# A graph layer on one core: the order of a load queue, of one rounding, and the engine that rounds the weights

## The chip, the core and the metric

The program runs on one core of a Trainium2 chip. The core has a matrix engine (TensorE, PE in the profile), three engines for work on whole tiles (VectorE is DVE, ScalarE is ACT, GpSimd is POOL) and SyncE (SP), which here only issues transfers. Each engine works through its own list in order; semaphores tie the lists together. Sixteen DMA engines move data between memory (HBM) and the on-chip buffers; the matrix engine writes into eight banks of PSUM. The metric is the device time of one execution in microseconds: of the kernel before, the median of 3 runs.

## What is computed

There are 16 batches, each with 512 nodes of 128 features (`x`) and a weighted adjacency matrix `adj` of 512x512. Seven relations are formed: the matrix, twice (relations 0 and 1), its transpose, twice (3 and 4), a shift by one node and its transpose (2 and 5), and the identity (6). The output is the largest of the seven, plus a bias and the input.

```python
h = jnp.maximum(_layernorm(x, axis=-1), 0.0)
...
HW = jnp.einsum('bnf,rfo->rbno', features, W[:, :F]) + jnp.einsum('rd,rdo->ro', W_edges, W[:, F:])[:, None, None, :]
AHW = jnp.einsum('rbnm,rbmo->rbno', A, HW)
out = jnp.max(AHW, axis=0) + b
return out
```

The term of `W_edges` is one vector per relation, c. Under a matrix A it becomes the row sums (or, for the transpose, the column sums) of A times c.

## The kernel before, in words

Every fp32 product is made of three products of rounded parts: each operand is split into a rounded `hi` and the rest `lo`, and `passes` (L847 to L849) multiplies hi by hi, lo by hi, hi by lo. ACT makes nearly every `hi` (for A, A turned, h turned, and the two products `fwd` and `bwd`), DVE or GpSimd the `lo`. The weights of the seven relations have `w_hi` and `w_lo`: the first three places are those of relations 2, 5 and 6 (`EYE`), the other four those of `FWD` (0, 1) and `BWD` (3, 4).

For a batch, `fwd` is the product of the turned A with h and `bwd` that of A with h, each over four chunks of 128 nodes. The three relations of `EYE` need only the turned h. The four others are finished a batch later, within the next batch's work (`along`, on PE): ACT first fills a bank with the sums of A times c (`fill`, L492), and the product with the weights is added onto it. DVE joins each finished relation into `best` (L669, L672), the first one by ACT (`join_first`, L500); then `best` is turned back and GpSimd adds bias and input.

The sums of A come as a by-product of ACT's rounding, as columns. PE turns them (L844), ACT writes them into `sum_rows` (`take_sums`, L487), SP stores them in memory (`store_sums`, L258, 4 KB) and reads them back spread over all 128 partitions (`spread_sums`, L264, 512 KB into `sum_all`). `fill` waits for this spread. There are two sets of buffers; batch b uses set b mod 2, and (k, q) in the code is batch 2k + q.

SP's queue carries all that is loaded in the regular part: x of a later batch (L212, 256 KB), the same x by blocks of 32x32 (`xp_sb`, L216, four transfers of 64 KB), blocks of the last column chunk of A (`a_blocks`, L216, four of 64 KB), A itself (`reload_a`, L245, two of 512 KB, for the batch two later), and the stores of the result (L221, four of 64 KB). The order is written out by hand: `first_steps` for batches 0 and 1, then `step` for every batch.

The order of ACT's and GpSimd's work is written out by hand as well, in a `first_step` (batch 0) and a `step` with special cases for batch 1 (`second`). In batch 1's step ACT rounds `bwd` of batch 0 only behind two fills and the normalisation of batch 2 (L462). The weights are rounded by ACT in `first_step` (L504), in two pieces, and split by GpSimd (L377).

Of the kernel before, what the change touches and what calls it, by code (L numbers as in the profile page):

```python
# [6 lines left out]
def gnn_layer(nc, x, adj, W, W_edges, bias, out):  # L7
# [15 lines left out]
    ACT = mybir.ActivationFunctionType  # L23
# [23 lines left out]
    with ctx:  # L47
# [162 lines left out]
        def _(sp):  # L210
# [22 lines left out]
            def load_xp(k, q):  # L233
                wait(sp, xb_ready, 2 * k + q - 1)
                load_by_blocks(xp_sb[q], x[2 * k + q, :, :], xp_loaded[q])
# [13 lines left out]
            def load_a_blocks(k, q):  # L249

                b = 2 * k + q
                wait(sp, a_turned[C - 1], b - 3)
                load_by_blocks(a_blocks[q], adj[b, :, (C - 1) * P:], a_blocks_loaded[q])

            def store_sums(k, q):

                sp.wait_ge(sum_rows_ready, 2 * k + q + 1)
                sp.dma_start(sums_dram[q][:, :], sum_rows[q][:]).then_inc(sums_stored[q], 16)  # L258
# [20 lines left out]
            def first_steps():  # L279

                load_x(0, 0)
                load_a(0, 0, 1)
                load_a(0, 0, 3)

                sp.wait_ge(a_loaded[0][0], 16)
                load_x(0, 1)
                load_w(EYE[:1], w_loaded)
                load_w(EYE[1:], w_loaded)
                for j in range(C):
                    load_a(0, 1, j)  # L290
                load_w(FWD, w_rest_loaded)
                load_w(BWD, w_rest_loaded)
                reload_x(0, 0)
                reload_a(0, 0)
                store_sums(0, 0)
                load_a_blocks(1, 0)
                spread_sums(0, 0)
                reload_x(0, 1)
                load_by_blocks(bias_sb, bias, bias_loaded)
                load_xp(0, 0)  # L300
                load_a_blocks(1, 1)
                load_xp(0, 1)
                store_sums(0, 1)
                reload_a(0, 1)
                spread_sums(0, 1)

            def step(k, q, more):

# [26 lines left out]
        def _(pool):  # L335
# [36 lines left out]
                wait(pool, out_stored[q], G * 16 * k)  # L372
                pool.tensor_tensor(o_sb[q][:], turned[q][:], xb_sb[q][:], ALU.add).then_inc(out_ready, 1)  # L373

            def split_w(n, places):
                pool.wait_ge(w_hi_ready, n + 1)
                pool.tensor_tensor(w_lo[:, places, :], w_sb[:, places, :], w_hi[:, places, :].bitcast(fp32),  # L377
                                   ALU.subtract).then_inc(w_lo_ready, 1)

            def first_step():  # L380
                ahead = (0, 1)
                split_a(0, 0, 2)
                split_a(0, 0, 3)
                reciprocal_std(*ahead)
                split_w(0, slice(0, W_EYE))
                split_h(*ahead)

            def step(k, q, left):
                if is_batch(2 * k + q, 1):
                    split_w(1, slice(W_EYE, R))  # L390
                    reciprocal_std(*after(k, q))
                    split_a(k, q, 0)
                    split_a(k, q, 1)
                    split_a(k, q, 2)
                    split_a(k, q, 3)
                    pool.wait_ge(bias_loaded, G * 16)
                else:
                    if left:
                        reciprocal_std(*after(k, q))
                    split_a(k, q, 2)  # L400
                    split_a(k, q, 3)
                    finish(k - 1, q)
                add_bias(*before(k, q))
                if left:
                    ahead = after(k, q)
                    split_h(*ahead)
                    split_a(*ahead, 0)
                    split_a(*ahead, 1)
# [23 lines left out]
        def _(act):  # L432
# [45 lines left out]
            def round_bwd(k, q):  # L478
                b = 2 * k + q
                act.wait_ge(bwd_done, b + 1)  # L480
                wait(act, rel_done[BWD[-1]], b)
                act.activation(bwd_hi[:], bwd_ps[:], ACT.Copy).then_inc(bwd_hi_ready, 1)
# [17 lines left out]
                act.activation(best[q][:], rel_bank(b, r)[:], ACT.Identity,  # L500
                               bias=c_col[:, r:r + 1]).then_inc(joined[r], 1)

            def round_w(places):
                act.activation(w_hi[:, places, :], w_sb[:, places, :], ACT.Copy).then_inc(w_hi_ready, 1)  # L504

            def first_step():
                ahead = (0, 1)
                act.wait_ge(w_loaded, 2 * 16)
                round_w(slice(0, W_EYE))
                take_sums(0, 0, rel_ps[1])  # L510
                round_at(*ahead, 0)
                round_at(*ahead, 1)
                normalise(*ahead)
                round_fwd(0, 0)
                act.wait_ge(c_ready, 1)
                join_first(0, 0)
                round_at(*ahead, 2)
                round_ht(*ahead)
                act.wait_ge(w_rest_loaded, 2 * 16)
                round_w(slice(W_EYE, R))  # L520
                round_at(*ahead, 3)
                round_a(*ahead, 0)
                round_a(*ahead, 1)

            def step(k, q, left):
                b = 2 * k + q
                prev = before(k, q)
                second = is_batch(b, 1)
                if not second:
                    round_at(k, q, 2)  # L530
                    round_at(k, q, 3)
                join_first(k, q)
                if not second:
                    take_sums(k, q)
                if second:
                    act.wait_ge(joined[EYE[1]], b)
                else:
                    act.wait_ge(joined[BWD[0]], b - 1)
                fill(*prev, FWD[0], rel_ps[BANK[FWD[0]]], filled[FWD[0]])
                act.wait_ge(joined[EYE[0]], b + 1)  # L540
                fill(*prev, FWD[1], rel_ps[BANK[FWD[1]]], filled[FWD[1]])
                if left:
                    ahead = after(k, q)
                    normalise(*ahead)
                if second:
                    round_bwd(*prev)
                    round_a(k, q, 2)
                    round_a(k, q, 3)
                act.wait_ge(joined[FWD[0]], b)
                fill(*prev, BWD[0], rel_ps[BANK[BWD[0]]], filled[BWD[0]])  # L550
                if left:
                    round_at(*ahead, 0)
                    if second:
                        take_sums(k, q, rel_ps[1])
                else:
                    round_fwd(k, q)
                act.wait_ge(joined[FWD[1]], b)
                fill(*prev, BWD[1], rel_ps[BANK[BWD[1]]], filled[BWD[1]])
                if left:
                    round_at(*ahead, 1)  # L560
                    round_ht(*ahead)
                    round_fwd(k, q)
                    for j in range(C):
                        round_a(*ahead, j)
                    round_bwd(k, q)
# [458 lines left out]
```

## Time and profile before

| | before |
|---|---|
| runs | 217.28, 215.5, 214.74 us; median 215.5 |
| profiled execution | 218.58 us, of which the span is 216.7 |
| PE busy | 205.2 us (95%) |
| DVE busy | 187.9 us (87%) |
| ACT busy | 186.6 us (86%) |
| GpSimd busy | 171.7 us (79%) |
| mean granted clock of PE | 0.985 |
| moved by DMA | 42.38 MB, mean 196 GB/s |

The profile is of one execution. Times in its rows count from the start of its span, in us. The granted clock is the share of 2.4 GHz that PE was given: 1.00, or 0.50, which is 1.2 GHz, and values between are means over a stretch. What a row has in brackets is the engine's idle time just ahead of the first instruction in it, and what ended it. A transfer's "landing" is the time from its issue to its arrival. The median lies 3.1 us below the profiled execution.

### The profile page before, as it was taken

How to read it: one execution, taken by the hardware profiler on the slowest of the kernel's cores; microseconds unless marked ns; L12 is line 12 of the kernel's file. 1: busy time of each engine (PE TensorE's matmuls, PEld its weight loads, DVE VectorE, ACT ScalarE, POOL GpSimd, SP SyncE). 2: the span in 40 equal slices, each digit the busy share in tenths (PEclk: the TensorE clock that was granted, in tenths of full speed). 3: DMA queues.
4: the chain of work that ended last, by engine and by line, in shares of the span. 5: the costliest groups of instructions: out<-in, count | busy, mean ns of one | idle time of the engine just before them, and what ended most of it. 6: DMA issues, size and time to landing. Idle time of an engine off the chain costs nothing.

```text
span 216.7 us, 4978 instructions
## 1 busy us (share of the span) xinstructions
PE 205.2 (95%) x1013; PEld 167.0 (77%) x1013; DVE 187.9 (87%) x400; ACT 186.6 (86%) x469; POOL 171.7 (79%) x181
## 2 busy tenths in 40 slices
PE   7799989799999999999999999999999999999980
PEld 5588865587888888788888888888888888888860
DVE  4798399389899989899899989999899989979783
ACT  4799887698999999999999999999999999999550
POOL 1566879829799797979899797979889797979341
PEclk9999999699999999999999999999999999999997
DMA  6997879796897989989888989899897989062726
GB/s 226 313 304 169 118 143 292 97 316 129 230 219 178 249 145 297 169 246 193 214 234 156 269 149 327 154 308 170 260 198 177 259 177 245 8 153 38 165 33 93
DMA packets 120320, 42.38 MB, mean 196 GB/s; under 512 B 100743, under 2 KB 110071, under 8 KB 120311
## 3 DMA queue, kind: packets, MB, share of 16 engines
q1 hardware_dynamic: 118688, 41.57, 80.0%
q10 hardware_dynamic: 1623, 0.71, 1.2%
q8 instruction: 3, 0.05, 0.1%
q14 instruction: 6, 0.05, 0.1%
HBM read 38.00 MB, written 4.26 MB: 195 GB/s over the span
## 4 chain that ended last, share of the span: by engine, by line
PE 79%; DMA 7%; SPq 5%; DVE 3%; ACT 2%; POOL 1%; issue 1%; DVEq 0%; ACTq 0%; POOLq 0%
PE rel_ps L849 11%; PE rel_ps L847 10%; PE rel_ps L848 10%; PE at_ps L821 8%; PE bwd_ps L847 6%; PE bwd_ps L849 6%; PE bwd_ps L848 6%; PE fwd_ps L847 6%; PE fwd_ps L849 6%; PE fwd_ps L848 6%; SPq L216 5%; DMA sum_all<-sums_dram 3%; DMA sums_dram<-sum_rows 3%; PE turn_ps L832 3%; DMA x_sb<-in_x 1%
## 5 line engine op out<-in xcount | busy, mean ns | idle before, releaser
L351 POOL TENSOR_TENSOR a_lo<-a_sb,a_hi 128x512 fp32r<-128x512 f32 x62 | 81.1, 1328 | 23.1 <-ACT a_hi L439 23.1
L672 DVE TENSOR_TENSOR best<-rel_ps,best 128x512 f32<-128x512 f32 x62 | 42.4, 684 | 6.8 <-PE rel_ps L849 5.7
L492 ACT ACTIVATE rel_ps<-sum_all,c_col 128x512 f32<-128x512 f32 (+1 forms) x63 | 41.6, 673 | 6.7 <-DVE best L672 4.1
L439 ACT ACTIVATE a_hi<-a_sb 128x512 fp32r<-128x512 f32 x64 | 39.6, 633 | 2.1 <-DMA a_sb<-in_adj 2.1
L643 DVE TENSOR_TENSOR at_lo<-at_ps,at_hi 128x512 fp32r<-128x512 f32 x48 | 32.8, 686 | 3.3 <-ACT at_hi L452 2.5
L452 ACT ACTIVATE at_hi<-at_ps 128x512 fp32r<-128x512 f32 x48 | 28.3, 591 | 5.0 <-PE at_ps L821 5.0
L847 PE MATMUL bwd_ps<-a_hi,h_hi 128*128 128x512 f32 x64 | 26.6, 416 | 1.4 <-DVE h_hi L760 0.8
L366 POOL TENSOR_TENSOR xb_sb<-xp_sb,bias_sb 128x512 f32<-128x512 f32 x16 | 23.0, 1436 | 5.2 <-DMA xp_sb<-in_x 5.2
L847 PE MATMUL fwd_ps<-at_hi,h_hi 128*128 128x512 f32 x64 | 26.8, 419 | 0.0
L821 PEld LDWEIGHTS at_ps<-ident,a_sb 128*128 128x128 f32 x184 | 22.2, 142 | 4.2 <-issue 0.2
L849 PE MATMUL fwd_ps<-at_hi,h_lo 128*128 128x512 f32 x64 | 25.4, 397 | 0.0
L821 PE MATMUL at_ps<-ident,a_sb 128*128 128x128 f32 x184 | 25.3, 273 | 0.0
L669 DVE SCALAR_TENSOR_TENSOR best<-rel_ps,c_col,best 128x512 f32<-128x512 f32 x32 | 23.8, 744 | 1.7 <-PE rel_ps L849 1.5
L848 PE MATMUL fwd_ps<-at_lo,h_hi 128*128 128x512 f32 x64 | 25.2, 394 | 0.0
L849 PE MATMUL bwd_ps<-a_hi,h_lo 128*128 128x512 f32 x64 | 25.2, 394 | 0.0
L848 PE MATMUL bwd_ps<-a_lo,h_hi 128*128 128x512 f32 x64 | 25.0, 391 | 0.0
L462 ACT ACTIVATE h_sb<-x_sb,shift,rstd 128x128 f32<-128x128 f32 x60 | 24.6, 479 | 0.0
L359 POOL TENSOR_TENSOR h_lo<-h_sb,h_hi 128x512 fp32r<-128x512 f32 x15 | 19.4, 1295 | 2.9 <-DVE h_hi L637 2.9
L847 PE MATMUL rel_ps<-ht_hi,w_hi 128*128 128x512 f32 x48 | 20.2, 421 | 0.0
L373 POOL TENSOR_TENSOR o_sb<-turned,xb_sb 128x512 f32<-128x512 f32 x15 | 19.7, 1315 | 0.0
L849 PE MATMUL rel_ps<-ht_hi,w_lo 128*128 128x512 f32 x48 | 19.0, 396 | 0.0
L848 PE MATMUL rel_ps<-ht_lo,w_hi 128*128 128x512 f32 x48 | 19.0, 395 | 0.0
(105 smaller groups left out, 471.7 us busy)
## 6 DMA issues: line engine op xcount, KB each, us to landing
a_sb<-in_adj SPq DMA_DIRECT2D x28, 512.0 KB, 4.2
sum_all<-sums_dram SPq DMA_DIRECT2D x16, 512.0 KB, 5.7
x_sb<-in_x SPq DMA_DIRECT2D x16, 256.0 KB, 5.0
xp_sb<-in_x SPq DMA_DIRECT2D x64, 64.0 KB, 2.9
out<-o_sb SPq DMA_DIRECT2D x60, 64.0 KB, 4.8
a_blocks<-in_adj SPq DMA_DIRECT2D x56, 64.0 KB, 2.3
a_sb<-in_adj SPq DMA_DIRECT2D x6, 256.0 KB, 4.3
a_sb<-in_adj ACTq DMA_DIRECT2D x2, 256.0 KB, 3.7
```

The costliest lines, as they stand in the source:

```text
L351: pool.tensor_tensor(a_lo[q][:, j, :], a_sb[q][:, j, :], a_hi[q][:, j, :].bitcast(fp32), ALU.subtract).then_inc(a_lo_ready[j], 1)
L439: act.activation(a_hi[q][:, j, :], a_sb[q][:, j, :], ACT.Copy, accum_out=sums[q][:, 0, j:j + 1]).then_inc(a_hi_ready[j], 1)
L452: act.activation(at_hi[q][:, i, :], at_from(b, i)[:], ACT.Copy, accum_out=sums[q][:, 1, i:i + 1]).then_inc(at_hi_ready[i], 1)
L462: last = act.activation(h_sb[q][:, j, :], x_sb[q][:, j, :], ACT.Relu, bias=shift[q][:, j:j + 1], scale=rstd[q][:, j:j + 1])
L492: act.activation(to[:, cols], sum_all[q][:, 0 if r in FWD else 1, cols], ACT.Copy, scale=c_col[:, r:r + 1]).then_inc(after_it, 1)
L643: dve.tensor_tensor(at_lo[q][:, i, :], at_from(b, i)[:], at_hi[q][:, i, :].bitcast(fp32), ALU.subtract).then_inc(at_lo_ready[i], 1)
L669: dve.scalar_tensor_tensor(out=best[q][:], in0=held[:], scalar=c_col[:, r:r + 1], in1=best[q][:], op0=ALU.add, op1=ALU.max).then_inc(joine ...
L672: dve.tensor_tensor(best[q][:], held[:], best[q][:], ALU.max).then_inc(joined[r], 1)
L821: last = pe.transpose(at_from(b, i)[:, j * P:(j + 1) * P], a_sb[q][:, j, i * P:(i + 1) * P], ident[:])
L847: pe.matmul(out, w_hi_, m_hi, start=start, stop=False, skip_group_check=onto)
L848: pe.matmul(out, w_hi_, m_lo, start=False, stop=False, skip_group_check=onto)
L849: return pe.matmul(out, w_lo_, m_hi, start=False, stop=stop, skip_group_check=onto)
```

## The change

Three edits are made, all for batches 0 and 1.

1. In SP's `first_steps`, the store of batch 1's sums goes ahead of the blocks of batch 3, and the spread ahead of the reload of A for batch 3; the load of xp of batch 1 goes last.
2. In ACT's step of batch 1, the rounding of batch 0's `bwd` moves from behind the fills and the normalisation to just behind the first join of batch 1.
3. The two roundings of the weights move from ACT to GpSimd, where each stands directly ahead of the split that uses it; GpSimd takes over the wait for the load.

```diff
@@ SP, first_steps
                 load_xp(0, 0)
+                store_sums(0, 1)
                 load_a_blocks(1, 1)
+                spread_sums(0, 1)
+                reload_a(0, 1)
                 load_xp(0, 1)
-                store_sums(0, 1)
-                reload_a(0, 1)
-                spread_sums(0, 1)
@@ GpSimd
-            def split_w(n, places):
+            def split_w(n, places, loaded):
+                pool.wait_ge(loaded, 2 * 16)
+                pool.tensor_copy(w_hi[:, places, :], w_sb[:, places, :]).then_inc(w_hi_ready, 1)
                 pool.wait_ge(w_hi_ready, n + 1)
                 pool.tensor_tensor(w_lo[:, places, :], w_sb[:, places, :], w_hi[:, places, :].bitcast(fp32),
                                    ALU.subtract).then_inc(w_lo_ready, 1)
...
-                split_w(0, slice(0, W_EYE))
+                split_w(0, slice(0, W_EYE), w_loaded)
...
-                    split_w(1, slice(W_EYE, R))
+                    split_w(1, slice(W_EYE, R), w_rest_loaded)
@@ ACT, first_step
-            def round_w(places):
-                act.activation(w_hi[:, places, :], w_sb[:, places, :], ACT.Copy).then_inc(w_hi_ready, 1)
-
...
-                act.wait_ge(w_loaded, 2 * 16)
-                round_w(slice(0, W_EYE))
                 take_sums(0, 0, rel_ps[1])
...
                 round_ht(*ahead)
-                act.wait_ge(w_rest_loaded, 2 * 16)
-                round_w(slice(W_EYE, R))
@@ ACT, step
                 if second:
+                    round_bwd(*prev)
                     act.wait_ge(joined[EYE[1]], b)
...
                 if second:
-                    round_bwd(*prev)
                     round_a(k, q, 2)
                     round_a(k, q, 3)
```

SP's queue, at the end of `first_steps` (`sums_dram<-sum_rows` is the store of the sums, `sum_all<-sums_dram` the spread, all three from batch 1; `a_blocks` and `a_sb` are for batch 3; the first `xp_sb` is batch 0's, the last batch 1's):

```order
 L216 DMA xp_sb<-in_x 32x16x32 x4
+L258 DMA sums_dram<-sum_rows 8x128
 L216 DMA a_blocks<-in_adj 32x16x32 x4
+L264 DMA sum_all<-sums_dram 128x1024
+L245 DMA a_sb<-in_adj 128x2x512 x2
 L216 DMA xp_sb<-in_x 32x16x32 x4
-L258 DMA sums_dram<-sum_rows 8x128
-L245 DMA a_sb<-in_adj 128x2x512 x2
-L264 DMA sum_all<-sums_dram 128x1024
```

The store has moved past two groups of four transfers, the spread past xp and A, and A past xp.

ACT's list before, from the rounding of h turned for batch 1 to the fill of the first bank of batch 0's transposed relations (`best1` is batch 1's join, `rel_ps` the banks filled with batch 0's sums, `h_sb0` batch 2's normalisation):

```order
22 L470 ACTIVATE ht_hi1<-turn_ps 128x512
23 L504 ACTIVATE w_hi<-w_sb 128x512
24 L452 ACTIVATE at_hi1,sums1<-at_ps1 128x512
25 L439 ACTIVATE a_hi1,sums1<-a_sb1 128x512 x2
26 L500 ACTIVATE best1<-rel_ps0,c_col 128x512
27 L492 ACTIVATE rel_ps2<-sum_all0,c_col 128x512
28 L492 ACTIVATE rel_ps0<-sum_all0,c_col 128x512
29 L462 ACTIVATE h_sb0<-x_sb0,shift0,rstd0 128x128 x4
30 L482 ACTIVATE bwd_hi<-bwd_ps 128x512
31 L439 ACTIVATE a_hi1,sums1<-a_sb1 128x512 x2
32 L492 ACTIVATE rel_ps2<-sum_all0,c_col 128x512
```

And the same piece in the changed kernel:

```order
21 L472 ACTIVATE ht_hi1<-turn_ps 128x512
22 L454 ACTIVATE at_hi1,sums1<-at_ps1 128x512
23 L441 ACTIVATE a_hi1,sums1<-a_sb1 128x512 x2
24 L502 ACTIVATE best1<-rel_ps0,c_col 128x512
25 L484 ACTIVATE bwd_hi<-bwd_ps 128x512
26 L494 ACTIVATE rel_ps2<-sum_all0,c_col 128x512
27 L494 ACTIVATE rel_ps0<-sum_all0,c_col 128x512
28 L464 ACTIVATE h_sb0<-x_sb0,shift0,rstd0 128x128 x4
29 L441 ACTIVATE a_hi1,sums1<-a_sb1 128x512 x2
30 L494 ACTIVATE rel_ps2<-sum_all0,c_col 128x512
```

The rounding of the weights is gone, and `bwd_hi` has moved ahead of two fills and the normalisation. The roundings of the weights now stand in GpSimd's list as `CAST w_hi<-w_sb`, of 128x384 and 128x512, each ahead of `w_lo<-w_sb,w_hi`.

## Rows read from the trace of the kernel before

**Rows 1.** Busy us (count) by stretch; then granted clock, DMA share, GB/s:

```profile
40.00:50.00 10.00, 10.00 (x47) 8.21 (x46) 7.40 (x19) 7.87 (x22) 5.62 (x7) 0.84 0.83 215
50.00:100.00 50.00, 50.00 (x254) 41.23 (x253) 46.76 (x98) 46.97 (x119) 44.51 (x46) 1.00 0.89 210
```

**Rows 2.** Chain that ended last, pieces: start us, us, what:

```profile
31.84 6.56 DMA sum_all<-sums_dram
...
55.45 0.87 PE at_ps L821 x8
...
67.72 0.87 PE at_ps L821 x8
```

**Rows 3.** Timeline near 39 us: start, us, engine, line, operation:

```profile
38.49 1.30 ACT L492 ACTIVATE rel_ps<-sum_all,c_col 128x512 f32<-128x512 f32 x2 [2.03 <-DMA sum_all<-sums_dram]
...
39.23 0.50 PE L847 MATMUL rel_ps<-fwd_hi,w_hi 128*128 128x512 f32 x1 [1.77 <-ACT rel_ps L492]
```

**Rows 4.** Timeline, 21 to 30 us, of ACT, DVE and PE:

```profile
21.23 0.69 ACT L500 ACTIVATE best<-rel_ps,c_col 128x512 f32<-128x512 f32 x1
...
25.23 0.69 DVE L660 TENSOR_TENSOR bwd_lo<-bwd_ps,bwd_hi 128x512 fp32r<-128x512 f32 x1 [3.36 <-ACT bwd_hi L482]
...
27.81 0.69 ACT L492 ACTIVATE rel_ps<-sum_all,c_col 128x512 f32<-128x512 f32 x1 [1.38 <-DVE best L672]
...
28.55 0.50 PE L847 MATMUL rel_ps<-bwd_hi,w_hi 128*128 128x512 f32 x1 [0.77 <-ACT rel_ps L492]
...
29.01 0.25 ACT L487 ACTIVATE sum_rows<-rel_ps 8x128 f32<-8x128 f32 x1
```

**Rows 5.** Timeline: PE's first turns of A for batches 2 and 3:

```profile
25.19 1.04 PE L821 MATMUL at_ps<-ident,a_sb 128*128 128x128 f32 x8
...
42.86 1.17 PE L821 MATMUL at_ps<-ident,a_sb 128*128 128x128 f32 x8
```

**Rows 6.** Timeline, 13 to 20 us, of the weights' splits and what is near:

```profile
13.51 1.01 POOL L377 TENSOR_TENSOR w_lo<-w_sb,w_hi 128x384 fp32r<-128x384 f32 x1
...
16.21 0.40 PE L847 MATMUL rel_ps<-ht_hi,w_hi 128*128 128x512 f32 x1
...
16.51 0.41 DVE L637 CAST h_hi<-h_sb 128x512 fp32r<-128x512 f32 x1
...
19.52 1.29 POOL L377 TENSOR_TENSOR w_lo<-w_sb,w_hi 128x512 fp32r<-128x512 f32 x1 [1.25 <-ACT w_hi L504]
```

**Rows 7.** Timeline of SP's queue: issue starts, and us until issued:

```profile
24.46 3.10 SPq L216 DMA_DIRECT2D a_blocks<-in_adj  x4
...
33.23 4.75 SPq L216 DMA_DIRECT2D xp_sb<-in_x  x4
...
43.14 0.39 SPq L264 DMA_DIRECT2D sum_all<-sums_dram  x1
...
46.48 2.61 SPq L212 DMA_DIRECT2D x_sb<-in_x  x1
...
92.98 0.35 SPq L264 DMA_DIRECT2D sum_all<-sums_dram  x1
```

**Rows 8.** Waits of SP, 45 to 60 us: total, times, longest:

```profile
SPq L264 <- DMA sums_dram<-sum_rows: 0.3, 1, 0.3
```

**Rows 9.** Landing (last column, us) of the spreads issued 17.71, 43.14, 92.98:

```profile
sum_all<-sums_dram SPq DMA_DIRECT2D x1, 512.0 KB, 4.0
...
sum_all<-sums_dram SPq DMA_DIRECT2D x1, 512.0 KB, 6.1
...
sum_all<-sums_dram SPq DMA_DIRECT2D x1, 512.0 KB, 6.7
```

**Rows 10.** Timeline: use of the sums of batches 2 and 6:

```profile
52.18 1.28 ACT L492 ACTIVATE rel_ps<-sum_all,c_col 128x512 f32<-128x512 f32 x2
...
101.25 1.28 ACT L492 ACTIVATE rel_ps<-sum_all,c_col 128x512 f32<-128x512 f32 x2
...
102.27 0.39 PE L847 MATMUL rel_ps<-fwd_hi,w_hi 128*128 128x512 f32 x1
```

## What I expected, written before the changed kernel ran

> **What bounds the kernel now.** I read the page's busy times, the table of stretches, the chain that ended last, and then the timeline at the one place where that chain leaves the matrix engine. PE is busy for 95% of the span, and from 50 to 100 us for every microsecond, at the full clock [rows 1]. One batch follows another every 12.27 us (PE's turns of A start at 55.45 and at 67.72 [rows 2]). So from batch 2 on (batches count from 0) the kernel runs at PE's pace, and what PE loses before that shows in full at the end. The chain names the loss: the spread sums of batch 1 are issued at 31.84 and land 6.56 us later [rows 2]. ACT waits 2.03 us for them and PE 1.77 us for ACT [rows 3]. A second loss follows: after this idle time PE works at 1.2 GHz. From 40 to 50 us the mean grant is 0.84 [rows 1], so 3.2 us of it were at a grant of 0.5, which cost 1.6 us; some of it lies just before 40, I take 1.75. A third lies ahead: DVE waits 3.36 us for `bwd_hi`, which ACT rounds late; DVE's joins are late by it, so ACT waits 1.38 us for the join before it fills a bank, and PE 0.77 us for that bank [rows 4].
>
> These come to 1.77 + 1.75 + 0.77 = 4.3 us. Another count: PE's turns of A start at 25.19 and 42.86 [rows 5], 17.67 us apart where the regular step is 12.27: 5.4 too long. I take 4.7, between the two.
>
> **The change part by part.**
>
> *bwd rounded first.* The product that is rounded has long been done. ACT can round it behind its first join of batch 1, which ends at 21.9 [rows 4], until 22.5; DVE's split moves from 25.23 to 22.5. From that split to the join that ACT waits for DVE needs 25.23 to 27.8 now [rows 4], 2.6 us, so the join is there at 25.1, or 25.4 since PE's product for it comes only then. ACT reaches the fill at 26.4, as early as it does now, and no longer waits: 1.3 us gained on ACT. `sum_rows` of batch 1, written from 29.01 to 29.26 now [rows 4], is there at 28.0. PE loses its 0.77. The price is 0.6 us on the fills of batch 0's forward banks, for the first of which PE then waits 0 to 0.1 us, and on the normalisation of batch 2, which PE's turns of A (from 25.19 [rows 5], 0.9 us of work) hide.
>
> *Weights rounded on GpSimd.* ACT loses two pieces of work of about 0.6 us. The first is worth nothing, as ACT then waits for PE's turned sums, the second little, as ACT then waits for PE's first relation of batch 1. GpSimd gets two CASTs, and no row of this kernel shows one. Bounds: DVE's cast of 128x512 takes 0.41 us, which scaled to 384 columns is 0.3; GpSimd's two-operand pass over the same 128x384 takes 1.01 [rows 6]. I take 0.8, nearer to the row of the same engine. It starts where that pass starts now, 13.51, so `w_lo` is ready at 13.51 + 0.8 + 1.01 + 0.1 = 15.4. PE's product is at 16.21, its weight load 0.2 before [rows 6]: hidden by 0.6 us, a stall from a cast of 1.4 us on. The second CAST, by the same bounds 0.4 to 1.35 us, falls into the 1.25 us that GpSimd now waits for ACT's rounding ahead of 19.52 [rows 6]: nothing.
>
> *The queue.* Before, SP issued blocks, xp, sums, A (2 x 512 KB), spread. Now it stands from 24.46 [rows 7], where it issued blocks, until `sum_rows` at 28.0; it issues the blocks by 30.5 and the spread at 30.6 instead of 31.84, with no A ahead. The spread took 6.56 us behind 1 MB of A [rows 2], and 4.0 for batch 0 without it [rows 9]. I take 4.3: landed at 34.9 instead of 38.4. ACT could have used it at 36.5 in the old kernel and is 1.0 ahead of that now, 35.5. **So the stall and the fall of the clock behind it go, and PE is 4.7 us ahead at batch 2.** A for batch 3 now goes at 31.2 behind the sums. PE turns it at 38.1 (42.86 less 4.7); with 0.5 MB ahead of it, it has 7 us. The batch 1 spread, with twice that ahead, took 6.56: I take no wait, up to 0.5 us as the bound.
>
> *What becomes late next.* SP's rows decide how much of the 4.7 stays. The spread of batch 2 is issued at 43.14 [rows 7] and takes 6.1 us [rows 9]: 49.24. The load of x behind it is issued at 46.48 and holds SP for 2.61 us, until 49.09 [rows 7], just when the spread has landed. Yet of waits for semaphores SP shows 0.3 us there [rows 8]. So SP is held by full queues, and its round is a loop of its own: spread landed, x, xp, blocks, sums, A, spread. It does not go faster because PE does. How far ahead is it? Batch 2's sums land at 49.24 and are used at 52.18 [rows 10]: 2.9 us. Batch 6's go at 92.98 [rows 7], land 6.7 later [rows 9] at 99.68, and ACT uses them at 101.25. Its two fills take 1.28, so the first ends at 101.9, and PE wants it at 102.27 [rows 10]: 1.57 + 0.35 = 1.92 us is all that PE can be ahead there, and it is the least of the batches that I read; for batch 2 it is 3.3. **So of 4.7 us 1.92 stay, plus what the queue itself gains.**
>
> That has bounds. If SP is never held, it issues x of batch 4 at 34.3, xp without the 4.75 us of [rows 7], and the spread of batch 2 at 41.0: 2.1 us earlier. If it is held as long as now, everything from x on is some 1.7 us later (it stands 3.6 us, and has 2 us of issues fewer in front of the sums). I take 0.4 us earlier, near the middle. **Kept: 1.9 + 0.4 = 2.3 us.** The profiled execution's own time, 218.58 us (span 216.7 and 1.9 around it), becomes 216.3. It lies 3.1 us above the median of the three runs, 215.5. I take the same 2.3 off that: 213.2, a ratio of 0.989. About 1% (213.35 to 217.65) is what a measurement of this kernel can tell from no change.
>
> By the rows of the spread, 6.56 behind A and 4.0 without, the transfers pass in order of issue. The Trainium skill has the rule ("DMA: Bandwidth & Descriptors", Queues, rings and completion order): on each DMA engine descriptors are consumed in ring order. By it whatever goes behind the sums pays for them, which speaks against a free gain; its result would be the 1.7 us bound, 215.3.
>
> **The rivals.**
> 1. *The queue keeps up* (17%). Against it: x's issue ends with the landing. For it: the DMA engines are busy for 0.89 of the time [rows 1], not all. Then 4.2 to 4.7 us stay: 210.8 to 211.3.
> 2. *The clock falls again* (12%). When PE catches up with the queue in batch 2, it idles 4.7 - 3.3 - 0.4 = 1.0 us, between the 0.77 us behind which the trace shows no slower product and the 1.77 us behind which it fell to 1.2. A fall costs 1.75 us, after which PE is late enough not to catch up soon: at worst 2.3 - 1.75 = 0.6 us kept, 214.9.
> 3. *The queue comes out late* (9%), at its bound: 1.9 - 1.7 = 0.2 us kept, 215.3.
> 4. *Slower* (7%): the cast is dear. Were it 4 us, `w_lo` would come at 18.6, PE would stall 2.6 us and probably run at half rate behind it (1.75 us more), and the sums and the queue would move by as much: 2.3 - 4.35 = 2.0 us lost, 217.5. It stalls from 1.4 us on; the sign turns at about 2 us with a fall of the clock, else at 3.7. For it speaks only that no row shows the operation. "GPSIMD Engine Reference" of the Trainium skill, Engine selection, says one-input operations run roughly at line rate there, which no row shows.
>
> **How the numbers follow.** The forecast has 55%, alone 211.8 to 214.9: the queue's move to either side of 0.4 by 1 us, and some noise. Faster by over 1%: its better part, 33%, and rival 1, 17%: 50%. Within 1%: its rest, 22%, and rivals 2 and 3: 43%. Slower by over 1%: 7%, the heavy forms of rival 4 and what I don't see. The range goes from rival 1's 210.8 to just above rival 3's, 215.5.
>
> **What would show it.** In the changed profile: DVE's split of bwd near 22.5, no wait of 1.38 us on ACT; `sum_rows` of batch 1 near 28.0; its spread issued near 30.6, landed near 35; a full clock and no idle PE from 35 to 45, and its turns of A near 38.2. Then ACT or PE waits for `sum_all` in batches 2 to 8, 0.2 to 1 us each, which were not there; SP's spread of batch 2 between 41.0 and 44.8. Wrong would be: CASTs over 1.4 us and a wait of PE for `w_lo`, a grant of 0.5 near 50 us, or no new wait for `sum_all` at all.

## The result, and the profile after

The change made the kernel slower: 219.96 us against 216.05 us, medians of four runs each (218.03 to 221.21 against 214.74 to 217.28), a ratio of 1.016 with an interval of 1.010 to 1.021. Forecast were 213.2 us and a gain of 1%. Ratios, here and below, are of fast runs: those over 1.5% above their kernel's fastest are left out, so that a ratio needn't be the quotient of the two medians.

The table sets beside each other the two profiled executions and the medians. It has a trap: both profiles lie off their kernel's middle, and in opposite directions. That of before, which the forecast read, lies 2.5 us over its median, that of after 1.9 us under its own. By the two profiles alone the change gains 0.5 us.

| | before | after |
|---|---|---|
| median of the runs | 216.05 us | 219.96 us |
| profiled execution, span | 218.58, 216.7 us | 218.03, 216.2 us |
| PE busy | 205.2 us | 203.9 us |
| clock of that execution | 0.985 | 0.998 |
| clocks of the changed kernel's other three runs | | 0.989, 0.983, 0.976 |

The stall of batch 1 is gone. This is the changed kernel's timeline, by the columns of [rows 3]: ACT fills the banks of batch 1 with no wait ahead of it, and PE turns A for batch 3.

```profile
35.98 1.28 ACT L494 ACTIVATE rel_ps<-sum_all,c_col 128x512 f32<-128x512 f32 x2
...
39.11 1.06 PE L816 MATMUL at_ps<-ident,a_sb 128*128 128x128 f32 x8
```

PE's turns come 3.75 us earlier than in [rows 5]. A batch later stands a longer stall than the one that went:

```profile
51.64 1.30 ACT L494 ACTIVATE rel_ps<-sum_all,c_col 128x512 f32<-128x512 f32 x2 [3.23 <-DMA sum_all<-sums_dram]
...
52.38 0.50 PE L842 MATMUL rel_ps<-fwd_hi,w_hi 128*128 128x512 f32 x1 [2.89 <-ACT rel_ps L494]
```

In the kernel before ACT used these sums at 52.18 without a wait [rows 10]. The chain that ended last (start, us, what) now goes through their spread, and then PE's beat takes over, 12.26 us where [rows 2] had 12.27. Ahead of the spread the chain runs through SP's own issues, so it is SP's queue and not an engine that sets the time there:

```profile
32.76 0.47 SPq L216
...
36.75 1.88 SPq L212
...
41.63 1.39 SPq L216
...
46.27 5.29 DMA sum_all<-sums_dram
51.64 0.70 ACT rel_ps L494
52.38 0.50 PE rel_ps L842
...
54.73 0.87 PE at_ps L816 x8
...
66.99 0.87 PE at_ps L816 x8
```

The stretches, with the columns of [rows 1], show PE idle for 2.4 us between 50 and 55 (and 0.5 just before), and the clock full in this execution:

```profile
40.00:50.00 10.00, 9.49 (x47) 7.43 (x45) 9.64 (x23) 7.81 (x22) 8.53 (x11) 1.00 0.86 192
50.00:55.00 5.00, 2.62 (x13) 2.18 (x14) 1.29 (x3) 3.36 (x7) 3.42 (x3) 1.00 1.06 233
```

The spread of batch 2 was issued at 43.14 before [rows 7], and is issued at 46.27 now. SP's queue in the changed kernel (issue starts, us until issued):

```profile
21.57 4.02 SPq L216 DMA_DIRECT2D xp_sb<-in_x  x4
28.90 0.28 SPq L258 DMA_DIRECT2D sums_dram<-sum_rows  x1
29.22 1.90 SPq L216 DMA_DIRECT2D a_blocks<-in_adj  x4
31.17 0.49 SPq L264 DMA_DIRECT2D sum_all<-sums_dram  x1
31.82 0.90 SPq L245 DMA_DIRECT2D a_sb<-in_adj  x2
32.76 3.60 SPq L216 DMA_DIRECT2D xp_sb<-in_x  x4
36.75 1.88 SPq L212 DMA_DIRECT2D x_sb<-in_x  x1
38.88 1.92 SPq L216 DMA_DIRECT2D xp_sb<-in_x  x4
41.10 3.33 SPq L216 DMA_DIRECT2D a_blocks<-in_adj  x4
44.49 0.38 SPq L258 DMA_DIRECT2D sums_dram<-sum_rows  x1
45.13 1.02 SPq L245 DMA_DIRECT2D a_sb<-in_adj  x2
46.27 0.39 SPq L264 DMA_DIRECT2D sum_all<-sums_dram  x1
```

From 25.59, where the first xp has been issued, to 28.90 SP stands, and the profile's waits of SP name what for:

```profile
SPq L258 <- ACT sum_rows L489: 3.3, 1, 3.3
```

Two theories were to be told apart. **The late queue**: the store stands ahead of eight transfers that were ready; while SP waits for the sums these aren't issued, and afterwards there is no slack in which to catch up, so the spread of batch 2 is late by that much. **The clock**: PE's new idle time makes the clock fall in most executions, and PE's half rate behind it is the loss. (In the expectations Q is the late queue, and E the rival that the edits of the engines bring the loss; L and C are the late queue alone, and the clock beside it.)

### The profile page after: what moved, and what is told of

It is laid out like the page before. It is cut to its first block, busy times and chain, and to the rows that moved or that the text cites. A ratio compares the mean times of both kernels' runs of the same rounds, so it can differ in the third digit from the quotient of the medians.

```text
span 216.2 us, 4978 instructions
## 1 busy us (share of the span) xinstructions
PE 203.9 (94%) x1013; PEld 166.3 (77%) x1013; DVE 188.3 (87%) x400; ACT 185.3 (86%) x467; POOL 172.5 (80%) x183
## 4 chain that ended last, share of the span: by engine, by line
PE 76%; SPq 7%; DMA 5%; DVE 4%; ACT 3%; issue 3%; ACTq 0%; DVEq 0%
PE rel_ps L842 10%; PE rel_ps L844 10%; PE rel_ps L843 10%; PE at_ps L816 8%; PE fwd_ps L842 6%; PE fwd_ps L844 6%; PE fwd_ps L843 6%; PE bwd_ps L842 6%; PE bwd_ps L844 6%; PE bwd_ps L843 6%; SPq L216 4%; PE turn_ps L827 3%; DMA sum_all<-sums_dram 2%; DMA a_sb<-in_adj 2%; SPq L212 1%
```

## The experiments

Ratios are to the kernel before on the same chip, with 95% intervals. "Store to spread" is the time on SP from the issue of batch 1's store to the issue of batch 2's spread. "Turns" is the start of PE's turns of A for batch 4. These two, the issue of the spread and the span are of one profiled execution, the median clock is that of all runs of the row. The clock of an execution also counts its last microseconds, in which PE has nothing left to do (from 210 us on 0.75 in the profile of before), so 0.990 is only a rough line between executions in which it fell in the work and those in which it didn't.

| kernel | median us | ratio | median clock | store | store to spread | spread of batch 2 | turns | span |
|---|---|---|---|---|---|---|---|---|
| before, profile of rows 1 to 10 | 216.05 | 1 | | 29.74 | 13.40 | 43.14 | 55.28 | 216.7 |
| `e11_before_again` | 216.52 (one run) | | 0.996 | 29.17 | 12.94 | 42.11 | 53.21 | 214.6 |
| after | 219.96 | 1.0157 (1.0100 to 1.0214) | 0.986 | 28.90 | 17.37 | 46.27 | 54.58 | 216.2 |
| `e3_changed_again` | 220.21 | 1.0137 (1.0082 to 1.0192) | 0.9865 | 27.55 | 18.06 | 45.61 | 56.55 | 218.9 |
| `e1_queue_alone` | 221.40 | 1.0126 (1.0083 to 1.0169) | 0.9885 | 29.04 | 18.20 | 47.24 | 57.88 | 219.3 |
| `e2_engines_alone` | 217.91 | 1.0032 (0.9996 to 1.0068) | 0.9865 | 29.53 | 13.42 | 42.95 | 55.45 | 216.9 |
| `e4_swap_only` | 217.03 | 0.9988 (0.9949 to 1.0028) | 0.9925 | 29.08 | 14.50 | 43.58 | 52.46 | 213.9 |
| `e5_no_wait_for_sums` | 216.55 | 0.9953 (0.9915 to 0.9991) | 0.9925 | 25.87 | 17.43 | 43.30 | 53.90 | 215.5 |
| `e6_xp_fills_the_wait` | 216.51 | 0.9996 (0.9956 to 1.0035) | 0.9915 | 27.66 | 14.95 | 42.61 | 51.79 | 214.2 |
| `e7_fill_idle_slots` | 215.56 | 0.9929 (0.9895 to 0.9962) | 0.993 | 29.47 | 13.89 | 43.36 | 52.61 | 214.1 |
| `e12_fill_again` | 215.68 | 0.9918 (0.9878 to 0.9958) | 0.992 | 29.96 | 14.34 | 44.30 | 53.67 | 215.1 |
| `e10_filled_old_engines` | 216.41 | 0.9977 (0.9950 to 1.0005) | 0.993 | 29.09 | 14.09 | 43.18 | 52.97 | 214.4 |
| `e9_changed_kept_warm` | 218.44 | 1.0114 (1.0074 to 1.0153) | 0.996 | 27.66 | 16.66 | 44.32 | 55.05 | 216.7 |
| `e8_xp_as_long_rows` | 215.94 | 0.9953 (0.9914 to 0.9993) | 0.994 | 29.44 | 15.85 | 45.29 | 54.24 | 215.7 |

One regularity helps in reading it: span less turns is 161.4 to 161.7 in twelve of the fourteen profiles, and 162.4 in the two others (`e3_changed_again`, `e6_xp_fills_the_wait`). From batch 4 on the kernel is nearly the same in all of them. What differs happens ahead of that.

### The parts apart

`e1_queue_alone` is the kernel before with edit 1, which is the changed kernel without edits 2 and 3; `e2_engines_alone` is the changed kernel with the old order in SP's queue:

```diff
@@ e1: the changed kernel, with the old ACT and GpSimd parts
-            def split_w(n, places, loaded):
-                pool.wait_ge(loaded, 2 * 16)
-                pool.tensor_copy(w_hi[:, places, :], w_sb[:, places, :]).then_inc(w_hi_ready, 1)
+            def split_w(n, places):
...
                 if second:
-                    round_bwd(*prev)
                     act.wait_ge(joined[EYE[1]], b)
...
@@ e2: the changed kernel, SP's first_steps
-                store_sums(0, 1)
                 load_a_blocks(1, 1)
-                spread_sums(0, 1)
-                reload_a(0, 1)
                 load_xp(0, 1)
+                store_sums(0, 1)
+                reload_a(0, 1)
+                spread_sums(0, 1)
```

> The kernel before with the new queue order alone; ACT and GpSimd as before. Theory Q (the loss sits in the queue: SP stands idle until the sums of batch 1 are there, and everything behind them, down to the spread of batch 2, goes about 3 us later, for which PE waits, and at times the clock falls too): sums of batch 1 stored at 29.3 to 29.8, spread of batch 1 at about 31.5, landing near 36 and hardly waited for; the spread of batch 2 issued at 46.5 to 47.5 instead of 43.1; PE waits 2.5 to 3.5 us for it near 50 us; time 1.01 to 1.02 of the kernel before. Theory E (the loss comes from the two edits of the engines: GpSimd's casts or ACT's new order): no loss, ratio 0.98 to 1.00.

> The changed kernel with the old queue order, so that only the rounding of bwd is moved and GpSimd rounds the weights. Theory Q: the 0.77 us of PE near 28 us go; the sums of batch 1 are stored 0.8 to 1.3 us earlier than 29.74 if SP is free by then, the spread still goes behind A and is waited for 1 to 2 us less than before; the spread of batch 2 is not later than 43.1; ratio 0.985 to 1.00. Theory E: ratio 1.01 to 1.02.

> The changed kernel itself, for a second trace and more clocks. Theory Q: again 1.01 to 1.02 of the kernel before; PE waits 2 to 4 us for the spread of batch 2; the executions differ by the clock they were granted behind that wait: span less (1 - clock) x span should be nearly the same in all, 213.5 to 216. If instead the loss comes from the first 12 us (in the profile of the changed kernel a split of DVE took 1.38 us beside a pass of GpSimd, and PE was 1.1 us late), the same 1.1 us must be there again.

Edit 1 alone brings the loss: 1.013, as much as the whole change in `e3_changed_again` (the same kernel once more; 1.014). By the medians of all runs it is 1.021 and 1.015. Its queue is the latest of all: SP is free at 23.39, stands 5.65 us until the store at 29.04, the spread of batch 2 goes at 47.24, and PE waits 3.5 us for these sums. The waits of `e1_queue_alone` from 30 to 60 us (total, times, longest):

```profile
ACT rel_ps L492 <- DMA sum_all<-sums_dram: 4.2, 2, 3.8
PE rel_ps L847 <- ACT rel_ps L492: 3.5, 1, 3.5
```

Edits 2 and 3 alone move nothing that can be measured, 1.003, which neither theory had. `sum_rows` is there at 27.44 in its profile, but the queue is the old one and SP reaches the store only at 29.53. The sums of batch 1 (spread at 31.25, behind A) landed as late as before, and PE now waits 3.6 us for them instead of 1.77. The clock fell behind this wait (0.71 from 40 to 45 us), and eight of the twelve executions are at 0.990 or below. An engine that is early at a late transfer has gained nothing.

`e3_changed_again` also settles a rival. In the profile of after a split of DVE near 9 us makes PE 1 us late (last section). In this one it doesn't, and the kernel is as slow. Its executions differ as expected by their clocks: span less (1 - clock) x span is 213.6 to 215.9 us in all six.

### Taking away the idle time of SP

In `e4_swap_only` the blocks and xp stand ahead of the store, as before the change, and only the spread goes ahead of A. In `e6_xp_fills_the_wait` xp alone is issued ahead of the store. In `e5_no_wait_for_sums` the order is that of the changed kernel, but the store takes a buffer of zeros that is ready long before, so SP has nothing to wait for; batch 1's sums are left out of its result.

```diff
@@ e4
                 load_xp(0, 0)
-                store_sums(0, 1)
                 load_a_blocks(1, 1)
+                load_xp(0, 1)
+                store_sums(0, 1)
                 spread_sums(0, 1)
                 reload_a(0, 1)
-                load_xp(0, 1)
@@ e6
                 load_xp(0, 0)
+                load_xp(0, 1)
                 store_sums(0, 1)
                 load_a_blocks(1, 1)
                 spread_sums(0, 1)
                 reload_a(0, 1)
-                load_xp(0, 1)
@@ e5
-                store_sums(0, 1)
+                sp.wait_ge(consts_ready, 1)
+                sp.dma_start(sums_dram[1][:, :], spare_rows[:]).then_inc(sums_stored[1], 16)
```

> The changed kernel, but in the queue blocks and xp go first, as before, and only the spread of batch 1 goes ahead of A. Theory Q: SP has work up to about 29.7, stores the sums then, waits about 2 us for them to be stored, spreads at 31.6 to 32 without A ahead (landing in about 4.3 us, near 36), and A follows; no wait of PE above 0.5 us in batch 1; the spread of batch 2 at 43.5 to 45, so a wait of 0 to 1.5 us in batch 2; ratio 0.985 to 1.0. Theory E: 1.01 or more.

> The changed kernel, with its queue order, but the store of batch 1's sums takes a buffer of zeros that is there from the start, so that SP does not wait for ACT (batch 1's sums are left out of the result). Only SP's idle time of 3.3 us at 25.6 to 28.9 is taken away. Theory Q (the idle time of SP is the loss): store at 25 to 26, spread of batch 1 near 28, the first A near 28 to 29 and the second near 30, when GpSimd has split batch 1's A; the spread of batch 2 issued at 43 to 44 instead of 46.3; wait of PE for it under 1 us; ratio 0.99 to 1.00. Theory O (it is the order, xp behind A, that makes the queue late, and not the idle time): spread of batch 2 at 45.5 or later, ratio 1.01 or more.

> The changed kernel with xp of batch 1 moved from the end of the five to their start: xp, sums, blocks, spread, A. SP then idles only about 1.3 us for the sums. Theory Q: the spread of batch 2 goes 1.5 to 2.1 us earlier than in the changed kernel, at 44.0 to 45.0, PE's wait for it is 1 to 2 us, ratio 1.000 to 1.008, halfway between the changed kernel and the one with the spread alone moved. Theory O: also earlier, but by less than 1 us.

All three take the loss away: the ratios are 0.999, 0.995 and 1.000, and the spread of batch 2 goes at 43.58, 43.30 and 42.61, in `e6_xp_fills_the_wait` earlier than was expected. `e5_no_wait_for_sums` is the cleanest of the three: same transfers in the same order, store to spread 17.43 us as in the changed kernel, 17.37. Only the 3.3 us in which SP stood are gone, and the spread is 2.97 us earlier. Against the expectation PE still waits 2.2 us for batch 2's sums, because it now comes to them early: its turns for batch 3 are at 37.77. The queue:

```profile
25.87 0.39 SPq L303 DMA_DIRECT2D sums_dram<-spare_rows  x1
...
43.30 0.39 SPq L265 DMA_DIRECT2D sum_all<-sums_dram  x1
```

How much of what SP stands comes out at the spread shows in the five profiles with this order. From the end of xp's issue to the store SP stood 0.0, 1.5, 2.6, 3.3 and 5.65 us (`e5_no_wait_for_sums`, `e9_changed_kept_warm`, `e3_changed_again`, after, `e1_queue_alone`), and the spread of batch 2 went at 43.30, 44.32, 45.61, 46.27 and 47.24. It follows the standing time with little given back up to 3.3 us, and with more behind that (in `e1_queue_alone` SP was also free 2 us earlier than in after).

The other column says how the store to spread time is made. With blocks and xp behind the store it is 16.7 to 18.2 us (five profiles, mean 17.5), with the blocks alone 14.95, with neither 12.9 to 15.9 (eight profiles, mean 14.1). So the two groups behind the store cost 3.5 us by the means, 4.0 between the profiles of before and after, and the store itself came only 0.3 to 2.2 us earlier in the two profiles of the changed kernel than in the two of the kernel before.

`e4_swap_only` keeps what was right in edit 1: with no A ahead of it the spread of batch 1, issued at 31.01, landed 4.2 us later, where 7.35 us passed in `e11_before_again` (issued 30.55, behind A). The waits for sums that were left in `e4_swap_only` are two of PE, 1.2 us together. Yet its ratio, 0.999, can't be told from the kernel before.

### Filling the idle time

`e7_fill_idle_slots` starts from `e4_swap_only`. In it SP stands 1.5 us between store and spread, waiting for the store to land. The loads of x for batches 3 and 4, which were ready, are put into these places: that for batch 3 into the same wait of batch 0's sums, that for batch 4 here. `e10_filled_old_engines` has this queue with the old ACT and GpSimd parts, `e12_fill_again` is the same kernel as `e7_fill_idle_slots`, on the chip of `e10_filled_old_engines`.

```diff
@@ SP, first_steps, against e4
                 load_a_blocks(1, 0)
-                spread_sums(0, 0)
                 reload_x(0, 1)
+                spread_sums(0, 0)
...
                 store_sums(0, 1)
+                reload_x(1, 0)
                 spread_sums(0, 1)
                 reload_a(0, 1)
@@ SP, step (batch 2's is written out ahead of the loop)
-                    reload_x(k, q)
+                    if not is_batch(2 * k + q, 2):
+                        reload_x(k, q)
```

> An attempt at a better order: as the kernel with only the spread moved ahead of A, but the load of x for batch 3 goes into SP's wait for the stored sums of batch 0 (15.9 to 17.7), and that of x for batch 4 into its wait for those of batch 1 (29.5 to 31.0). Theory Q: 0.9 us of issues leave the busy part of the queue; the spread of batch 1 lands 0.5 to 0.8 us later than 35.2, still in time or waited for by under 0.5 us; that of batch 2 goes at 42.3 to 43.2; ratio 0.990 to 0.998. If the DMA engines themselves and not SP's issues hold the queue, the spread of batch 2 stays at 43.3 to 43.8 and the ratio at 0.997 to 1.002.

> The order of the queue with its two idle slots filled, but ACT and GpSimd as in the kernel before. Theory Q (the queue alone decides, what the engines gain is eaten by it): ratio as that of the same queue with the new engine order, 0.990 to 0.996. Theory E2 (with the queue in time the earlier sums and the 0.77 us of PE count): 0.3 to 0.6% slower than that kernel, 0.996 to 1.000.

> The kernel with the filled queue and the new engine order once more, beside the same queue with the old engine order, on one chip: again 0.990 to 0.996 of the kernel before.

0.993 and 0.992, and both intervals exclude 1: this queue order beats the kernel before by 0.7 to 0.8% (by the medians of all runs 0.5% each), and the changed kernel by about 2%. PE's waits for sums in `e7_fill_idle_slots` from 30 to 60 us are small; ACT's are 0.30 us in batch 1 and 0.51 in batch 2:

```profile
36.44 1.30 ACT L498 ACTIVATE rel_ps<-sum_all,c_col 128x512 f32<-128x512 f32 x2 [0.30 <-DMA sum_all<-sums_dram]
...
49.67 0.69 ACT L498 ACTIVATE rel_ps<-sum_all,c_col 128x512 f32<-128x512 f32 x1 [0.51 <-DMA sum_all<-sums_dram]
```

How the gain comes about isn't shown. The spread of batch 2 was expected at 42.3 to 43.2 and goes at 43.36 and 44.30, where `e4_swap_only` has 43.58. In the profile of `e12_fill_again` PE even waits 1.1 us for batch 1's sums and 1.1 for A of batch 3, and its span is 0.5 us longer than that of `e11_before_again`. The gain stands in the medians and ratios only.

With the old engines it is 0.998, on the chip on which `e12_fill_again` gave 0.992. So edits 2 and 3 seem to be worth some 0.6% in this queue order, and nothing with the old one (`e2_engines_alone`). The two intervals overlap slightly (0.9950 to 0.9958), by the medians it is 0.3%, and the profiles don't show where it is won, so this is likely and not settled.

### The clock, or the queue?

`e9_changed_kept_warm` is the changed kernel with twelve products of zeros on PE, ahead of the product that waits for batch 2's sums. They add nothing to the result, and in its profile they take 2.9 us of an idle time of 4.6. To have them in one batch only, the first steps of PE's loop are written out.

```diff
                 fwd(k, q, 2)
+                if is_batch(b, 3):
+                    pe.wait_ge(sum_rows_ready, b + 1)
+                    for _ in range(12):
+                        pe.matmul(turn_ps[:], warm[:, 0:P], warm[:], start=True, stop=True)
                 along(*prev, FWD[0])
```

> The changed kernel with 12 products of a tile of zeros (about 2.8 us of PE) put ahead of the first product that waits for batch 2's sums, so that PE works through most of that wait; the result is untouched. Theory C (the loss is part late queue, part fall of the clock behind the new wait): the granted clock of its executions goes from a median of 0.986 back to 0.993 or more, the spread of batch 2 stays late (45.5 to 47.5), and the ratio falls from 1.014 to 1.003 to 1.009. Theory L (only the late queue costs, the lower clock is hidden because PE is ahead of the queue anyway): the ratio stays at 1.010 to 1.016.

The clock was mended: no execution of twelve was at 0.990 or below, where all six of `e3_changed_again` were. The time was hardly: 1.011 instead of 1.014, less than the clock's theory wanted and within the range of the late queue alone. PE still waits for sums that aren't there; `e9_changed_kept_warm`, by the timeline:

```profile
52.86 0.50 PE L842 MATMUL rel_ps<-fwd_hi,w_hi 128*128 128x512 f32 x1 [1.66 <-ACT rel_ps L494]
...
55.05 1.03 PE L816 MATMUL at_ps<-ident,a_sb 128*128 128x128 f32 x8
```

Against it `e3_changed_again`, whose clock fell, in the same places: the product at 52.55, the turns at 56.55, and the stretches by the columns of [rows 1]:

```profile
50.00:55.00 5.00, 2.45 (x6) 1.99 (x7) 0.77 (x2) 2.91 (x7) 2.14 (x2) 0.64 0.96 201
55.00:60.00 5.00, 5.00 (x23) 4.31 (x22) 2.45 (x7) 3.01 (x8) 1.27 (x1) 0.68 0.81 199
```

From the product to the turns it takes 4.0 us there, 2.2 in the profile of after and in `e9_changed_kept_warm`. So within batch 2 a fall costs 1.8 us, and the turns themselves are slow too (1.83 instead of 1.03 us), which is why this profile ends 0.9 us later than the others (162.4 instead of 161.4 to 161.7). The lateness itself, without a fall, is 54.58 or 55.05 less the 53.21 of `e11_before_again`: 1.4 to 1.8 us. By these profiles the fall costs more than the lateness. By the ratios, keeping the clock up gives back only 0.2% of the 1.4%, with intervals that overlap; by the medians of all runs 0.7% of 1.5% (1.008 against 1.015).

The runs of one kernel say the same without an added product. The three of `e1_queue_alone` at a clock of 0.997 took 218.1 to 219.2 us, the nine at 0.990 or below 220.3 to 223.8, and the kernel before had a median of 216.9 beside them. After at 0.998 took 218.03, its three others 219.6 to 221.2. What holds is that the late queue alone is enough for about 1%, and that in the executions in which the clock falls as well, some 1% comes on top, as far as runs that differ in more than their clock can tell. The exact share is open: the spread in the profile of `e9_changed_kept_warm` went at 44.32, earlier than was expected, and took 7.7 us where the other four with this order took 5.3 to 6.3, so the twelve products may not be without a price of their own, or that execution had a late transfer by chance.

### Packets or issues?

In `e8_xp_as_long_rows`, which starts from `e4_swap_only`, xp of batches 0 and 1 is loaded in rows of 2 KB instead of pieces of 128 B. It then stands in another layout, so right results of these two batches are left out. Were the small packets what fills the queue, it should be early.

```diff
-                load_xp(0, 0)
+                load_xp(0, 0, True)
                 load_a_blocks(1, 1)
-                load_xp(0, 1)
+                load_xp(0, 1, True)
                 store_sums(0, 1)
```

> The kernel with only the spread moved ahead of A, with xp of batches 0 and 1 loaded as rows of 2 KB instead of pieces of 128 B: the same bytes and as many transfers, but 16 times fewer packets (xp_sb of these two batches is then laid out wrongly, and so are their results). It asks whether packets or bytes and issues hold the queue. If packets: the spread of batch 2 goes 1 to 2 us earlier than 43.6, PE has no wait for it, ratio 0.985 to 0.995. If SP's issues: it goes at 43.2 to 43.8 and the ratio is 0.997 to 1.00.

It wasn't, in its profile: spread of batch 2 at 45.29, and PE stood 1.7 us before the turns at 40.12, where A had landed late. Its ratio is nevertheless low, 0.995. The profile is of one of its two slowest runs and doesn't point the same way as the ratio, so the run settles nothing.

## Why the prediction was wrong, step by step

**What bounds the kernel: right.** PE's pace held (12.26 us in the chain of after), and what was lost ahead of batch 4 stood in full at the end: span less turns moved by 0.3 us over twelve profiles whose turns lie up to 5.4 us apart.

**bwd first: right.** DVE's split came at 23.59 (forecast 22.5, in an execution that was 1.1 us late from a place at 9.3 us, below), and the waits of 1.38 and 0.77 us [rows 4] are gone:

```profile
23.59 0.69 DVE L655 TENSOR_TENSOR bwd_lo<-bwd_ps,bwd_hi 128x512 fp32r<-128x512 f32 x1 [0.56 <-ACT bwd_hi L484]
...
27.44 0.68 ACT L494 ACTIVATE rel_ps<-sum_all,c_col 128x512 f32<-128x512 f32 x1
...
28.62 0.25 ACT L489 ACTIVATE sum_rows<-rel_ps 8x128 f32<-8x128 f32 x1
```

`sum_rows` was forecast for 28.0 and is written at 28.62, in `e3_changed_again`, which lacks the 1.1 us, at 27.28. The split comes at 22.24 there.

**The CASTs: right, and cheaper than taken.** Taken were 0.8 us for the first, with 0.3 to 1.01 as bounds; it took 0.51, the second 0.61, and PE waited for neither. Rival 4, the dear cast, is refuted; the kernel came out slower by another way.

```profile
13.62 0.51 POOL L377 CAST w_hi<-w_sb 128x384 fp32r<-128x384 f32 x1
...
19.38 0.61 POOL L377 CAST w_hi<-w_sb 128x512 fp32r<-128x512 f32 x1
```

**The spread without A ahead: right.** Taken 4.3 us to its landing, measured 4.4 (31.17 to 35.57). Here the Trainium skill's rule that an engine's descriptors are consumed in ring order ("DMA: Bandwidth & Descriptors", Queues, rings and completion order) agrees with the traces: 7.35 us with 1 MB of A issued ahead in `e11_before_again`, 4.4 with none.

**The move of the queue: wrong, and this decides.** The step said that from the store at 28.0 the spread of batch 2 would come at 42.74, 0.4 us earlier than before, and at 44.84 in the worst case. That is 14.7 us from store to spread, 16.8 at worst. Measured were 17.4 and 18.1, against 13.4 before. The worst case had set the 3.6 us in which SP stands against "2 us of issues fewer in front of the sums", and had stopped there. But the blocks and xp don't go away. They come behind the store, and cost 1.90 and 3.60 us there, xp being held; x, the next xp and the next blocks follow at the old pace. In [rows 7] SP was held at batch 2's xp for 4.75 us, and the better case took it that this holding would shrink. Now batch 1's xp takes 3.60, x 1.88 and batch 2's xp 1.92: the hold of 4.75 us has moved ahead and is spread over more transfers, and the sum of these three is no smaller, 7.4 us against 7.2 before (2.09, 0.39 and 4.75). A queue that feeds transfer engines busy for 0.89 of the time [rows 1] has only the rest to catch up in: over the 17 us from store to spread an estimate of 1.9 us. Less still was caught up: of the 3.3 us of standing in after 3.0 came out at the spread, against `e5_no_wait_for_sums`. The forecast had the 0.89 before it, and used it only in rival 1. So the term of the queue, put at a gain of 0.4 us, was a loss of 3.1 in the two profiles that belong together (43.14 to 46.27), and of 2.5 to 4.2 over all pairs of the changed kernel's two profiles with the two of before. Up to 1.1 us of after's share is its late start. The loss met a margin of 3.3 us in batch 2 that was meant to be spent on PE's head start of 4.7. This margin was itself that of an execution in which PE had been slowed: in `e11_before_again` the spread of batch 2 lands at 49.4 and is used at 50.11, 0.7 us later and not 2.9. Rival 3, the queue comes out late, had the mechanism and the sign, with 9% and a bound of 1.7.

**The fall of the clock as a gain of 1.75 us: wrong.** It was in the profiled execution of before, but the kernel's executions mostly lack it: over the 29 to 35 executions that stood beside the experiments the median clock was 0.992 to 0.995, and 4 to 8 were at 0.990 or below. `e11_before_again` is the kernel before once more, run to see this: expected were the same wait of about 1.8 us, no fall behind it, and turns for batch 3 that start 1.5 to 2 us earlier. ACT waits 1.63 us for batch 1's sums and PE 1.38, no product slows down, and the turns start at 40.92 instead of 42.86, 1.94 us earlier:

```profile
38.73 0.50 PE L847 MATMUL rel_ps<-fwd_hi,w_hi 128*128 128x512 f32 x1 [1.38 <-ACT rel_ps L492]
...
40.92 1.04 PE L821 MATMUL at_ps<-ident,a_sb 128*128 128x128 f32 x8
```

So of the 4.7 us that were to be won, some 2 weren't there in most runs. The sum was made against 218.58 and then taken off a median 3.1 us lower, which still counted the fall in full.

**The clock falls again in batch 2: rival 2, and it came.** Its condition was an idle time of over 1 us; PE's was 2.9 and 4.0 us. Three of the four runs of after and all six of `e3_changed_again` have a clock of 0.990 or less. The weight of 12% was too small, because it rested on the queue being 0.4 us early.

**A for batch 3 with no wait: nearly.** Taken nothing, bound 0.5. In after there is none, in `e3_changed_again` 0.36 and in `e4_swap_only` 0.44 us before the turns. In other orders with the spread first it passes the bound: 0.78 us in `e1_queue_alone`, 1.1 in `e12_fill_again`.

**Waits for the sums in batches 2 to 8: mostly wrong.** In after there is the one of 2.9 us and none later, since PE, put back by it, doesn't reach the queue again. The cap of "1.92 us ahead" shows in one run: the turns of `e6_xp_fills_the_wait` come earliest, 1.4 us ahead of `e11_before_again`, and 1.0 us of that is gone by the end (162.4), with two waits of ACT for sums behind 60 us, 0.9 us together.

## What to carry to other kernels

Here a queue whose transfers kept the DMA engines busy for 0.9 of the time got back next to nothing of the 3.3 us that it stood. For such a queue: put work that is ready ahead of its waits, and count what you moved behind a wait in full, up to the next transfer that somebody waits for. A wait removed on an engine is worth what the next late transfer leaves of it; here the same engine edits were worth nothing behind a late queue and perhaps half a per cent in a filled one. And take no term from a single profiled execution that its own median doesn't bear out: look at the clocks of several executions before a fall of the clock is counted as something to win.

## What the runs showed of the hardware that was not expected

**The clock after an idle PE.** No length of the one wait separates the cases: the clock fell behind 1.77 us (before), 2.2 (`e5_no_wait_for_sums`, 0.66 from 50 to 55) and 3.5 to 4.0 us, and did not behind 1.38 (`e11_before_again`), 1.5 (`e6_xp_fills_the_wait`), 1.7 (`e8_xp_as_long_rows`) and 2.9 us (the profile of after). By their clocks, three other executions of that same kernel had it. What decides was not found.

**DVE beside GpSimd.** In the profiles of after and of `e7_fill_idle_slots` the last 128x128 split of h takes 1.38 us, where the same instruction takes 0.29 in the twelve other profiles. In both it starts 0.05 to 0.06 us behind a pass of GpSimd over 128x512; in `e3_changed_again` it starts ahead of that pass, at 9.01 against 9.17, and takes 0.29. The changed kernel:

```profile
8.84 0.29 DVE L760 TENSOR_TENSOR h_lo<-h_sb,h_hi 128x128 fp32r<-128x128 f32 x1
...
9.25 2.58 POOL L351 TENSOR_TENSOR a_lo<-a_sb,a_hi 128x512 fp32r<-128x512 f32 x2 [2.67 <-ACT a_hi L441]
9.31 1.38 DVE L760 TENSOR_TENSOR h_lo<-h_sb,h_hi 128x128 fp32r<-128x128 f32 x1
...
12.60 0.47 PE L842 MATMUL fwd_ps<-at_hi,h_hi 128*128 128x512 f32 x1 [0.99 <-DVE at_lo L638]
```

It delays PE by 1 us at 12.6. As it stands in code that the change doesn't touch and comes and goes between profiles, it is taken for chance, which is not shown. The Trainium skill ("SBUF — State Buffer", SBUF: two separate sides) states that a pass of DVE with two inputs in SBUF and a pass of GpSimd take one pair of ports in turn, each for its whole instruction. By it the split would wait from 9.31 for the end of GpSimd's first pass, half of the 2.58 us from 9.25 on, so until 10.54, and end 0.1 to 0.3 us behind that: the trace has 10.69. Both numbers agree with the rule, yet no run took the GpSimd pass away, so it is argued and not shown.
